# Bank-major matmul loops and softmax normalised in pairs of heads, in a kernel of scan layer and local attention on 8 cores

## What is computed

```python
f = tanh(x @ Wf.T); w = sigmoid(x @ Wi.T); c = silu(x @ Wv.T)
state = f_t * state + w_t * c_t              # over the 2048 tokens
x = layernorm(x + silu(states) @ Wo.T)
x1 = x
for l in range(2):                            # DEPTH
    h = shift_token(x)                        # upper half of the channels one token late
    q, k, v = split(h @ wqkv[l], 3)           # 8 heads of 64
    q = l2norm(q) * qs; k = l2norm(k) * ks; q, k = rotary_xpos(q, k)
    # window 512: each query block sees itself and at most 512 tokens back
    attn = softmax(8 * q @ k.T + mask); o = attn @ v
    x = x + o @ wo[l]
    h = layernorm(shift_token(x)) * lg + lb
    a, g = split(h @ w1[l] + b1, 2)           # 2 x 2730
    x = x + (a * gelu(g)) @ w2[l] + b2
y = layernorm(x1 + x)
```

## Time and profile before

| | |
|---|---|
| timed executions | 8896.05 and 9084.82 us, median 8990.43 |
| the profiled execution | 8800.55 us; span of its slowest core 8799.0 us |
| spans of the 8 cores in it | 8770.5 to 8799.0 us |
| TensorE busy | 57% of the span |
| VectorE busy | 37% |
| ScalarE busy | 25% |
| DMA | 50 GB/s of HBM traffic on average |

### The profile page before, as it was taken

One profiled execution on the slowest core, in us unless ns is written; L12 is line 12 of the kernel. 1 busy time (PEld: TensorE's weight loads), 2 busy tenths in 40 slices (PEclk: granted clock), 3 DMA queues, 4 the chain that ended last, 5 costly groups with the idle time before them and its releaser, 6 DMA issues.

```text
span 8799.0 us, 72013 instructions; the slowest of 8 cores (8770.5 to 8799.0 us)
## 1 busy us (share of the span) xinstructions
PE 4981.6 (57%) x19328; PEld 1973.4 (22%) x19328; DVE 3270.8 (37%) x5184; ACT 2227.1 (25%) x3898; POOL 620.7 (7%) x860
## 2 busy tenths in 40 slices
PE   4724445577834455579566244455786444556794
PEld 2201122233311122234122011222333111222341
DVE  1334444433134444432324344444321443443314
ACT  2311144311011244211133111443101113441111
POOL 0000000011200000012000000000111000001120
PEclk9855555588955555689687555555888555557896
DMA  3120000054510000246241200001545000003463
GB/s 61 17 80 5 6 2 1 8 49 47 83 17 5 4 1 1 20 46 69 61 102 14 81 5 7 1 1 11 47 54 86 6 5 4 1 1 29 46 70 90
DMA packets 582870, 273.54 MB, mean 31 GB/s; under 512 B 526389, under 2 KB 570202, under 8 KB 570202
## 3 DMA queue, kind: packets, MB, share of 16 engines
q0 software_dynamic: 550016, 168.06, 19.0%
q1 hardware_dynamic: 32474, 100.88, 3.2%
HBM read 403.32 MB, written 33.55 MB: 50 GB/s over the span
## 4 chain that ended last, share of the span: by engine, by line
PE 41%; DVE 25%; ACT 12%; DMA 10%; issue 10%; DVEq 1%; ACTq 0%; SPq 0%; POOLq 0%; POOL 0%
PE ps L329 19%; PE ps L298 11%; PE ps L339 10%; DMA a<-w 5%; DVE a L539 5%; DVE a L667 3%; ACT a L638 3%; DVE a L634 3%; ACT a L626 2%; DVE a L428 1%; ACT a L671 1%; DVE a L551 1%; DVE a L811 1%; DVE a L547 1%; DVE a L532 1%
## 5 line engine op out<-in xcount | busy, mean ns | idle before, releaser
L329 PE MATMUL ps<-a 128*128 128x512 bf16 (+1 forms) x9728 | 2322.2, 400 | 760.0 <-ACT a L729 229.3
L339 PE MATMUL ps<-a 128*128 128x128 bf16 (+5 forms) x4032 | 1461.2, 410 | 1577.8 <-DVE a L539 514.6
L298 PE MATMUL ps<-a 128*128 128x512 bf16 (+2 forms) x5568 | 1240.8, 371 | 1455.4 <-ACT a L671 746.6
L329 PEld LDWEIGHTS ps<-a 128*128 128x128 bf16 (+1 forms) x9728 | 985.4, 102 | 2093.3 <-issue 1099.2
L298 PEld LDWEIGHTS ps<-a 128*128 128x128 bf16 (+2 forms) x5568 | 542.5, 121 | 2167.1 <-issue 1849.8
L339 PEld LDWEIGHTS ps<-a 128*128 128x128 bf16 (+3 forms) x4032 | 445.6, 123 | 2539.4 <-issue 2499.0
L277 POOL DMA_DIRECT2D a<-w x704 | 494.2, 704 | 2102.6 <-DMA a<-w 882.4
L892 DVE SCALAR_TENSOR_TENSOR a<-ps,a 128x512 bf16<-128x512 f32 (+1 forms) x352 | 264.1, 750 | 1012.9 <-ACT a L886 981.4
L638 ACT ACTIVATE a<-a 128x640 f32<-128x640 f32 (+4 forms) x512 | 390.2, 762 | 492.2 <-DVE a L634 492.0
L634 DVE TENSOR_REDUCE a<-a 128x1 f32<-128x640 f32 (+4 forms) x512 | 376.8, 736 | 327.8 <-ACT a L626 324.5
L886 ACT ACTIVATE a<-ps,a 128x512 bf16<-128x512 f32 (+1 forms) x352 | 222.8, 684 | 963.0 <-PE ps L329 962.9
(11 more groups left out here) (57 smaller groups left out, 2624.7 us busy)
## 6 DMA issues: line engine op xcount, KB each, us to landing
a<-w POOLq DMA_DIRECT2D x336, 256.0 KB, 5.1
a<-w POOLq DMA_DIRECT2D x336, 128.0 KB, 3.1
a<-x SPq DMA_DIRECT2D x16, 1024.0 KB
x1sp<-a SPq DMA_DIRECT2D x16, 1024.0 KB
a<-x1sp SPq DMA_DIRECT2D x16, 1024.0 KB
y<-a SPq DMA_DIRECT2D x16, 1024.0 KB
a<-wqkv POOLq DMA_DIRECT2D x48, 256.0 KB, 4.2
a<-Wf POOLq DMA_DIRECT2D x16, 256.0 KB, 4.5
```

Of the source, the lines that this page charges most:

```text
L298: eng.matmul(o, lt, r, start=st, stop=sp)),
L329: eng.matmul(bank(bk, p0, p1), lt, r, start=st, stop=sp)),
L339: eng.matmul(o, lt, r, start=True, stop=True)),
```

## The change

1. In `ssm` (gates and Wo), q/k/v and the output projection `mm_kmajor` gives way to a loop over the banks: all k tiles of one bank (`mmg`), then its evacuation, then the next bank. The count and the sizes of the matmuls stay the same; their line is now that of `Group.member`. The output projection alternates between banks 0-3 and 4-7, q/k/v between [0, 1, 2, 3] and [6, 7, 2, 3].
2. `flush_pending` becomes a queue, called before the matmuls of m. For m < 8 it keeps one entry, which gives the same order as before; at m = 8 it empties, so that `proc_qk` of tile 7 is emitted before the matmuls of tile 8 instead of after them.
3. In attention the reciprocal is taken once for a pair (128 x 2), in the soft step of the odd unit, and both scalings L646 follow there, the even unit's first. `sim_f`, `exf` and `att_t` go from four buffers to two, `at_tp` to three.
4. One small DMA of 128 ones to a second partition of `oner` is added at the start, and the two SBUF areas change size slightly.

```diff
             for gi in range(3):
-                mm_kmajor(
-                    8,
...
-                    [0, 1, 2, 3] if gi % 2 == 0 else [4, 5, 6, 7],
...
+                bset = [0, 1, 2, 3] if gi % 2 == 0 else [4, 5, 6, 7]
+                for c in range(NC4):
+                    bk = bset[c]
+                    mmg([(bank(bk), tr.ap(0, 128, gi * CH + k * 128,
+                                          gi * CH + (k + 1) * 128),
+                          x_bf[k].ap(0, 128, c * CK, (c + 1) * CK)) for k in range(8)],
+                        (tr.key,) + tuple(x.key for x in x_bf), (f"ps{bk}",))
+                    vop(lambda eng, gi=gi, c=c, bk=bk: eng.activation(
                         outs[gi].ap(0, 128, c * CK, (c + 1) * CK), bank(bk), actf[gi]),
...
-            vop(lambda eng, h=h: eng.reciprocal(
-                smax.ap(0, 128, 8 + h, 9 + h), ssum.ap(0, 128, h, h + 1)),
-                reads=("ssum",), writes=("smaxr",))
-            vop(lambda eng, W=W, h=h, atp=atp, ex=ex: eng.activation(
-                atp.ap(0, 128, 0, W), ex.ap(0, 128, 0, W), AF.Copy,
-                scale=smax.ap(0, 128, 8 + h, 9 + h)),
-                reads=(ex.key, "smaxr"), writes=(atp.key,), eng="act")
+            if h % 2 == 1:
+                vop(lambda eng, h=h: eng.reciprocal(
+                    smax.ap(0, 128, 7 + h, 9 + h), ssum.ap(0, 128, h - 1, h + 1)),
+                    reads=("ssum",), writes=("smaxr",))
+                exp_ = exf[(i - 1) % 2]
+                atpp = at_tp[(i - 1) % 3]
+                vop(lambda eng, W=W, h=h, atpp=atpp, exp_=exp_: eng.activation(
+                    atpp.ap(0, 128, 0, W), exp_.ap(0, 128, 0, W), AF.Copy,
+                    scale=smax.ap(0, 128, 7 + h, 8 + h)),
+                    reads=(exp_.key, "smaxr"), writes=(atpp.key,), eng="act")
+                vop(lambda eng, W=W, h=h, atp=atp, ex=ex: eng.activation(
+                    atp.ap(0, 128, 0, W), ex.ap(0, 128, 0, W), AF.Copy,
+                    scale=smax.ap(0, 128, 8 + h, 9 + h)),
+                    reads=(ex.key, "smaxr"), writes=(atp.key,), eng="act")
...
+        def flush_pending(keep=0):
+            while len(pending) > keep:
+                m0 = pending.pop(0)
...
         for m in range(12):
+            flush_pending(keep=1 if m < 8 else 0)
...
-            flush_pending()
+            bset = [0, 1, 2, 3] if m % 2 == 0 else [6, 7, 2, 3]
+            for c in range(NC4):
+                bk = bset[c]
+                mmg([(bank(bk), ws.ap(0, 128, k * 128, (k + 1) * 128),
+                      h_bf[k].ap(0, 128, c * CK, (c + 1) * CK)) for k in range(8)],
+                    (ws.key,) + tuple(h.key for h in h_bf), (f"ps{bk}",))
+                qkv_evac(c, bk)
...
-        sim_f = [AL.buf(F32, 640, f"simf{i}") for i in range(4)]
-        exf = [AL.buf(F32, 640, f"exf{i}") for i in range(4)]
-        at_tp = [AL.buf(BF16, 640, f"attp{i}") for i in range(4)]
-        att_t = [AL.buf(BF16, 640, f"att_t{i}") for i in range(4)]
+        sim_f = [AL.buf(F32, 640, f"simf{i}") for i in range(2)]
+        exf = [AL.buf(F32, 640, f"exf{i}") for i in range(2)]
+        at_tp = [AL.buf(BF16, 640, f"attp{i}") for i in range(3)]
+        att_t = [AL.buf(BF16, 640, f"att_t{i}") for i in range(2)]
...
-                [0, 1, 2, 3],
-                lambda k, ws=ws: (ws.key,) + tuple(o.key for o in o_bf),
...
+            bset = [0, 1, 2, 3] if m % 2 == 0 else [4, 5, 6, 7]
+            for c in range(NC4):
+                bk = bset[c]
+                mmg([(bank(bk), ws.ap(0, 128, k * 128, (k + 1) * 128),
+                      o_bf[k].ap(0, 128, c * CK, (c + 1) * CK)) for k in range(4)],
+                    (ws.key,) + tuple(o.key for o in o_bf), (f"ps{bk}",))
```

More of the change, by code:

```diff
@@ L33 @@
 QCLS = {"syncq": "sq", "poolq": "pq"}
-F32_COLS = 27360
-BF_COLS = 51680
+F32_COLS = 27312
+BF_COLS = 51776
 class Plan:
@@ L485, in ssm @@
             for gi in range(3):
[L486 to L493 removed]
+                bset = [0, 1, 2, 3] if gi % 2 == 0 else [4, 5, 6, 7]
[6 more added lines that the diff above has]
+                    vop(lambda eng, gi=gi, c=c, bk=bk: eng.activation(
                         outs[gi].ap(0, 128, c * CK, (c + 1) * CK), bank(bk), actf[gi]),
[L495 removed]
+                        reads=(f"ps{bk}",), writes=(outs[gi].key,), eng="act")
             vop(lambda eng: eng.tensor_tensor(fgb.ap(), fgb.ap(), fgc.ap(), OP.mult),
@@ L506, in ssm @@
                 WoT[:, :, ht * 128:(ht + 1) * 128], (), (tr.key,))
[L507 to L513, removed]
+            bset = [0, 1, 2, 3] if ht % 2 == 0 else [4, 5, 6, 7]
+            for c in range(NC4):
+                bk = bset[c]
+                mmg([(bank(bk), tr.ap(0, 128, k * 128, (k + 1) * 128),
+                      s_bf[k].ap(0, 128, c * CK, (c + 1) * CK)) for k in range(8)],
+                    (tr.key,) + tuple(s.key for s in s_bf), (f"ps{bk}",))
+                vop(lambda eng, ht=ht, c=c, bk=bk: eng.tensor_tensor(
                     x_cm[ht].ap(0, 128, 1 + c * CK, 1 + (c + 1) * CK),
@@ L516, in ssm @@
                     bank(bk), OP.add),
-                    reads=(f"ps{bk}", f"x{ht}"), writes=(f"x{ht}",)))
+                    reads=(f"ps{bk}", f"x{ht}"), writes=(f"x{ht}",))
         outer_ln(None)
@@ L601, in emit_soft @@
             W = n * 128
-            sf = sim_f[i % 4]
-            ex = exf[i % 4]
-            atp = at_tp[i % 4]
+            sf = sim_f[i % 2]
+            ex = exf[i % 2]
+            atp = at_tp[i % 3]
             def pch(c):
@@ L658, in emit_tail @@
             W1 = min(W, 512)
-            atp = at_tp[i % 4]
-            att = att_t[i % 4]
+            atp = at_tp[i % 3]
+            att = att_t[i % 2]
             for c in range(n):
@@ L720, in ffn_layer @@
         wqs = [AL.buf(BF16, CH, "wqs0")]
-        qraw = [AL.buf(F32, S, "qraw0"), AL.buf(F32, S, "qraw1")]
+        qraw = [AL.buf(F32, S, f"qraw{i}") for i in range(2)]
         vcm = AL.buf(BF16, CK, "vcm")
@@ L725, in ffn_layer @@
         rotb = sqb
-        rota = [AL.buf(F32, CK, "rota0"), AL.buf(F32, CK, "rota1")]
+        rota = [AL.buf(F32, CK, f"rota{i}") for i in range(2)]
         for t in range(NT):
@@ L732, in ffn_layer @@
         wq = wqkv[l].rearrange("(k p) n -> p k n", p=128)
[L733 to L737, removed]
+        pending = []
+        def flush_pending(keep=0):
+            while len(pending) > keep:
+                m0 = pending.pop(0)
                 if m0 < 4:
@@ L770, in qkv_evac @@
                             reads=(f"ps{bk2}",), writes=(v_tm[t].key,))
[L771 to L774, removed]
-                [0, 1, 2, 3],
-                lambda k, ws=ws: (ws.key,) + tuple(h.key for h in h_bf),
-                qkv_evac)
-            flush_pending()
+            bset = [0, 1, 2, 3] if m % 2 == 0 else [6, 7, 2, 3]
[5 more added lines that the diff above has]
+                qkv_evac(c, bk)
             if m < 8:
-                pending[0] = m
+                pending.append(m)
         flush_pending()
@@ L804, in ffn_layer @@
                 wo_r[:, :, m * 128:(m + 1) * 128], (), (ws.key,))
[L805 to L809, removed]
-                lambda k, ws=ws: (ws.key,) + tuple(o.key for o in o_bf),
-                lambda c, bk, m=m: vop(lambda eng, m=m, c=c, bk=bk: eng.tensor_tensor(
+            bset = [0, 1, 2, 3] if m % 2 == 0 else [4, 5, 6, 7]
+            for c in range(NC4):
+                bk = bset[c]
+                mmg([(bank(bk), ws.ap(0, 128, k * 128, (k + 1) * 128),
+                      o_bf[k].ap(0, 128, c * CK, (c + 1) * CK)) for k in range(4)],
+                    (ws.key,) + tuple(o.key for o in o_bf), (f"ps{bk}",))
+                vop(lambda eng, m=m, c=c, bk=bk: eng.tensor_tensor(
                     x_cm[m].ap(0, 128, 1 + c * CK, 1 + (c + 1) * CK),
@@ L814, in ffn_layer @@
                     bank(bk), OP.add),
-                    reads=(f"ps{bk}", f"x{m}"), writes=(f"x{m}",)))
+                    reads=(f"ps{bk}", f"x{m}"), writes=(f"x{m}",))
         AL.release()
```

2 lines of the change are left out of this document (1 added, 1 removed).

## The result

The changed kernel takes 9413.6 us in the median of its timed runs (9302.8 to 9639.9), the kernel before, timed again beside it, 8852.5 (8795.5 to 9084.8). The ratio is 1.0576, with a 95% interval of 1.0509 to 1.0643: slower by 5.8%. The profiled execution has a span of 9315.7 us against 8799.0, 517 us more.

A forecast was written before the change was run, and what follows sets the result against it. No engine was full; in attention, the largest touched stage, a ring through TensorE, VectorE and ScalarE bound the pair. Terms +627 +64 -50 -5 -24 -85 = +527 us, put on 8896, gave 9420 us (ratio about 1.059), range 9180 to 9680.

The forecast's parts named there:

- Attention, +627 forecast: Attention: the even unit's later scaling delays its transposes and copy, 157 us a layer, 627 us in four layers.
- +2.73: Attention, pairs with n = 5: even unit's reciprocal-to-copy path grows from 0.10 to 2.83 us, making the pair 12.7 us.
- my line through n = 3 and 5: Attention, pairs with n = 1 to 4: mean loss of 1.6 us, from 1.83 at n = 3 and 2.73 at n = 5.
- Gates of the scan, -50: Scan gates: evacuating each bank once full removes TensorE's stop between tiles, 3.1 us a tile, 50 us in all.
- The rival of a falling clock: Scan layer: denser matmuls lower their own clock, 67 us lost in place of 55 gained, total +649; chance 0.03.
- v tiles, +64: q/k/v: v matmuls in bursts of 8 run at a lower clock, +4.0 us a tile over 16 tiles.
- TensorE waits in each round as before: v tiles: each round after 8 matmuls costs TensorE 2.5 us, with the number of waits unchanged.
- q and k tiles, -24, bounds 0 and -40: q/k/v: earlier evacuations gain 10 us a layer, bank 6 waits and tile 7's move cost some; net -6 a layer.
- Output projection, -85: Output projection: two sets of banks end the waits for VectorE, 54.7 to 32 us, 85 us in four layers.
- TensorE staying slow: v tiles and output projection: TensorE keeps its low clock, total +628, 9524 us; chance 0.18.
- Transposes partly hidden: Attention: the even unit's transposes partly overlap other work, half of the 627 us, total +214, 9110 us; chance 0.06.
- VectorE set free: Attention: removing the even reciprocal's wait frees VectorE, up to 287 us saved, total -387, 8509 us; chance 0.04.

The follow-up runs named there:

- e1: The kernel before with only the attention part (paired reciprocal and scalings, fewer buffers): span 9371.5 to 9387.7 us, pair 12.68 us.
- e4: The changed kernel with the odd unit's scaling before the even unit's: span 9442 to 9447 us, pair 13.39 us.
- e7: The changed kernel with a unit's transposes into one bank issued without waiting for each other: span 8896 us, pair 10.94 us.
- e12: The changed kernel with only each unit's tail emitted one round later: span 8462 to 8479 us, pair 9.3 us.
- e2: The changed kernel with attention and its buffers as before the change: span 8676 us, ratio 0.9845 to the kernel before.
- e5: e2 with the four v tiles back in the k-major loop in banks 0 to 3: span 8569 us.
- e6: e2 with weights of v tiles loaded a tile ahead, into a table tile no longer read: span 8634 us, ratio 0.9796.
- e9: e2 with the pair's output copy emitted after the next unit's row maximum: span 8317 us, pair 8.45 us.
- e10: e2 with a unit's transposes into one bank unbroken: span 8648 us, pair 9.78 us.
- e8: e2 combined with the edits of e5, e7 and e9, and q and k in banks 0 to 3 only: span 8101 us.

## Why the prediction was right

The forecast was 9420 us and a ratio of about 1.059; measured are 9414 and 1.058. The main mechanism was right, and e1, e4, e7 and e12 show it part by part; that the total came so close is partly luck, as the terms and the base show.

- **Attention, +627 forecast.** For n = 5 the step is as forecast: +2.73, measured 12.68 - 9.96 = 2.72. The term for n = 1 to 4 was too high: the steps are 0.8, 1.0, 1.7 and 2.5 us, and the first 16 pairs take 127.8 us for 104.6, 1.45 each in place of 1.6. With n = 1 and 2 the even reciprocal, not TensorE, had released the odd copy, and taking it away gave some back (n = 1: from the even to the odd copy 1.26 us in place of 1.66), more than my line through n = 3 and 5 said. From first to last row maximum the four layers grew by 149 us each (mean), 597 in all. The tail of the last unit lies behind that and adds 2.8 a layer: the projection's first add comes 13.1 us after the last row maximum, in e2 10.3. Together about 608.
- **Gates of the scan, -50, and Wo, -5.** 768 matmuls now take 168.1 us, where they stretched from 107.65 to 301.46, 193.8: 26 us a sequence, 51 in all. The first q matmul comes 30 us earlier (550.5 for 580.5, medians of the cores), so it is 60 for both terms. The rival of a falling clock is out: from 114 to 272 us all eight cores show a granted clock of 1.00. The limiter that the Trainium skill describes (TensorE: Matmul & The Clock Gate, Seeing it yourself) did not show here; the measurement decides.
- **v tiles, +64.** About 96 by e5. The clock's part came out as forecast: a layer's v matmuls are busy for 52.3 us in place of 37.2 (means), 3.8 a tile, 60 in all. The Trainium skill (TensorE: Matmul & The Clock Gate, A second HAM failure mode: psum-queue depth-cycling) describes a clock that goes to and fro between bursts; the trace agrees, with groups of 3.62 and 1.89 us. What was wrong is the step "TensorE waits in each round as before". The v tile's weights have a single buffer, free only when the tile's last matmul has ended. Before, 10 us of rounds stood behind it and hid the load; now only the last round of 2.5 us does, and TensorE waits for the DMA, 6.7 us a layer. The prediction allowed for late weights in the projection, not here. With the slower matmuls that come behind it, the wait is worth about 40 us of the 96 (e6).
- **q and k tiles, -24, bounds 0 and -40.** From the first to the seventh long reciprocal the four layers take 9.6 us less each (317.5 for 327.1 in the mean), and 2 us less from the first q matmul to the first long reciprocal: some -46, outside the bounds. The squares start 0.58 us after the matmuls instead of 2.2, as forecast. What the term left out: the 32 matmuls of even tiles, bank by bank, took 8.8 us (median) instead of 9.7. Those of odd tiles, with the wait for bank 6, stayed at 9.6. Tile 2's matmuls, and the first square behind its last copy:

```profile
616.57 8.72 PE L298 MATMUL ps<-a 128*128 128x512 bf16 x32
...
625.87 0.63 ACT L528 ACTIVATE a<-a 128x512 bf16<-128x512 f32 x1
```

- **Output projection, -85.** 54.7 us became 33.8 (1822.22 to 1855.99), 21 a layer, 84 in all, at a clock of 0.96 for 0.87. I had 32; the weights were late by 0.66 to 1.15 us four times.
- **The small DMA**, taken as nothing: the first matmul starts between 103 and 110 us on the cores of the kernel before and between 104 and 114 in the changed one, so no cost is seen above their spread.
- **Sum.** 608 + 96 - 60 - 46 - 84 = 514; measured 517 between the slowest cores, 507 between cores in the middle (9295 and 8788). The errors of the terms, -19, +32, -5, -22 and +1, nearly cancel, so the closeness of the total is partly luck.
- **The base.** I put the change on 8896, a single timed run. The kernel before, timed more often, has its median at 8853 and its lowest run at 8796; the changed one 9414 and 9303. On the lowest run the forecast would have been 9323, 20 us too much; that 9420 meets the median within 6 us is luck.
- **The rivals.** TensorE staying slow: true for most of the v tiles, false in the projection. Transposes partly hidden: out by the 3.92 us of idle TensorE. VectorE set free: not so in this order, but e9 shows that VectorE's waits were worth a look, for the output copy rather than the reciprocal.

## What to carry to other kernels

In a software pipeline of in-order engines, first write down the ring: for one period, which instruction releases which, back to its own successor. An instruction that is moved behind a later event costs the whole chain from that event to its consumer if the consumer is on the ring, however little work it is; moving the consumer by one round as well (e12) took it away here. Batching two small operations saves nothing where neither was on the ring. And when a loop order is changed, look at every single-buffered load whose cover was the work that now comes earlier.

## What was not expected of the hardware

- A matmul that waits for the end of the one before it into the same bank costs 0.41 us a step with 128 columns at the half clock; unbroken, four weight loads take 0.35 us in all (e7). Removing these waits took 420 us from the changed kernel, where they are on the ring, and 28 us from the run without the attention part, where they mostly are not (e10).
- A wait of one or two us in front of a dense group can cost more than its length. In the changed kernel the 32 matmuls of the odd q and k tiles, which wait for bank 6, take 9.6 us (median), those of the even ones 8.8; in e8, without that wait, the odd ones take 8.5 too. The v tiles without the weight wait save 10 us a layer where the waits are 6.8. Why the kernel before, k-major and without such a wait, needed 9.5 to 9.7 for most tiles was not tried and stays open.
- Dense matmuls of 512 columns on all eight cores at once kept a granted clock of 1.00 from 114 to 272 us (768 of them took 168 us).
